# Slot attention of a two-layer decoder on one core: units of four heads, projection weights cut into fp32r parts, masks and scales moved from VectorE to ScalarE and GpSimd

## The reference, cut to what matters

```python
h = layernorm(x)
q, k = rope(h @ Wq.T), rope(h @ Wk.T)        # 16 heads x 128
v, g = h @ Wv.T, h @ Wg.T                    # 16 heads x 128
s = clip(h @ Ws1.T @ Ws2.T + bs2, -32, 32)   # 16 heads x 64 slots
z = cumlogsumexp(s, over time); es = exp(s); enz = exp(-z)
A = where(mask, q @ k.T * DK**-0.5, 0)
ok = enz * (A @ es)
qv = softmax(ok)
W2 = where(mask, (qv * enz) @ es.T, 0)
o = W2 @ v
x = x + (o * rsqrt(mean(o*o) + eps) * g_norm * silu(g)) @ Wo.T
```

## Time and profile before

| | |
|---|---|
| times of three runs | 2183.06, 2193.24, 2196.49 us (median 2193.24) |
| the profiled execution | 2183.35 us, span 2181.5 us |
| PE busy in the span | 1842.2 us, 84% |
| DVE busy | 1384.4 us, 63% |
| ACT busy | 763.0 us, 35% |
| POOL busy | 338.7 us, 16% |

### The profile page before, as it was taken

The page is one execution under the profiler, slowest core; times in us unless marked ns, Lnnn a source line. Parts: engine busy times, 40 slices in busy tenths (PEclk is TensorE's granted clock), DMA queues, the critical chain, the costliest instruction groups (busy, mean ns, idle before and its releaser), DMA issues.

```text
span 2181.5 us, 30632 instructions
## 1 busy us (share of the span) xinstructions
PE 1842.2 (84%) x11622; PEld 1096.2 (50%) x11622; DVE 1384.4 (63%) x3057; ACT 763.0 (35%) x1191; POOL 338.7 (16%) x507
## 2 busy tenths in 40 slices
PE   6998898898875559898998988997697598999977
PEld 3677777676763213343433435564354244444446
DVE  6766675775644546778677834343556687888843
ACT  1122122122121204545545561342122155556652
POOL 1311111111202100102011003242110011311110
PEclk9999999999996759999999997999798799999989
DMA  6000000000007270722707207363712136465200
GB/s 223 1 1 1 1 1 1 0 1 0 1 1 184 98 97 31 122 30 88 95 30 125 28 2 293 126 215 130 128 35 38 44 42 117 74 96 68 28 1 20
DMA packets 86747, 142.91 MB, mean 66 GB/s; under 512 B 14229, under 2 KB 56345, under 8 KB 86602
## 3 DMA queue, kind: packets, MB, share of 16 engines
q1 hardware_dynamic: 72418, 116.12, 25.7%
q10 hardware_dynamic: 12312, 19.71, 3.2%
q0 software_dynamic: 1872, 5.13, 0.6%
HBM read 108.35 MB, written 32.03 MB: 64 GB/s over the span
## 4 chain that ended last, share of the span: by engine, by line
PE 61%; DVE 19%; DMA 7%; issue 6%; ACT 3%; SPq 2%; POOL 1%; ACTq 1%; another core or an unknown queue 0%; POOLq 0%; DVEq 0%
PE bank L1054 8%; PE bank L1014 7%; PE bank L1033 6%; PE bank L1369 5%; PE bank L1704 5%; PE bank L556 4%; PE bank L625 3%; PE bank L1723 2%; PE bank L547 2%; DVE xa_part_max L1127 2%; PE bank L599 2%; PE bank L2113 2%; DMA xa_k_parts<-xa_parts 1%; DMA xa_qst<-xa_q_parts 1%; DVE gsa_enz L716 1%
## 5 line engine op out<-in xcount | busy, mean ns | idle before, releaser
L1127 DVE TENSOR_REDUCE xa_part_max<-bank 128x1 f32<-128x448 f32 (+1 forms) x512 | 273.8, 569 | 85.7 <-PE bank L1014 80.5
L1088 ACT ACTIVATE xa_e<-bank 128x1024 f32<-128x1024 f32 (+1 forms) x208 | 212.5, 1022 | 145.1 <-PE bank L1033 143.0
L1088 ACT ACTIVATE ca_e<-bank 128x1024 f32<-128x1024 f32 (+2 forms) x208 | 196.4, 956 | 102.4 <-PE bank L1033 93.8
L1127 DVE TENSOR_REDUCE ca_part_max<-bank 128x1 f32<-128x400 f32 (+1 forms) x384 | 205.9, 570 | 36.6 <-PE bank L1014 32.8
L1014 PE MATMUL bank<-xa_kst,xa_qst 122*128 122x448 bf16 (+1 forms) x512 | 172.0, 361 | 48.9 <-issue 24.9
L1014 PE MATMUL bank<-ca_kst,ca_qst 125*128 125x400 bf16 (+2 forms) x512 | 161.2, 351 | 25.5 <-DMA ca_qst<-ca_q_parts 11.8
L1033 PE MATMUL bank<-xa_qst,xa_kst 128*128 128x256 bf16 (+1 forms) x832 | 129.8, 279 | 21.5 <-DMA xa_qst<-xa_negT 21.5
L1054 PE MATMUL bank<-xa_e,xa_vaug 128*17 128x256 f32 (+2 forms) x1792 | 142.8, 394 | 1.0 <-ACT xa_e L1088 0.6
L1054 PE MATMUL bank<-ca_e,ca_vaug 128*17 128x256 f32 (+2 forms) x1664 | 126.2, 376 | 8.9 <-ACT ca_e L1088 8.0
L813 POOL TENSOR_TENSOR gsa_qk<-gsa_qk,gsa_rot 128x512 f32<-128x512 f32 x64 | 82.8, 1294 | 298.8 <-DVE gsa_rot L727 298.8
L1014 PEld LDWEIGHTS bank<-xa_kst,xa_qst 122*128 122x128 bf16 x512 | 48.8, 99 | 159.0 <-DVE xa_part_max L1127 83.9
(11 more groups left out here) (337 smaller groups left out, 3528.3 us busy)
## 6 DMA issues: line engine op xcount, KB each, us to landing
xa_kst<-xa_k_parts SPq DMA_DIRECT2D x96, 200.1 KB, 8.8
ca_kst<-ca_k_parts SPq DMA_DIRECT2D x96, 200.1 KB, 7.5
xa_k_parts<-xa_parts SPq DMA_DIRECT2D x8, 1200.8 KB, 6.0
ca_k_parts<-moe_ctx_parts SPq DMA_DIRECT2D x8, 1200.8 KB
moe_gu<-in_expert_gate_up SPq DMA_DIRECT2D x8, 1024.0 KB
shared<-in_ctxT_split ACTq DMA_DIRECT2D x4, 1601.0 KB, 7.8
moe_ctxT<-in_ctxT SPq DMA_DIRECT2D x8, 800.5 KB, 8.0
ca_cv<-in_ctx ACTq DMA_DIRECT2D x4, 1536.0 KB
```

The costliest lines, as they stand in the source:

```text
L1088: e.activation(self.e[m % 3][0:rows, :, first:T], banks[m % 2][0:rows].rearrange("p a (h t) -> p (a h) t", t=T)[:, :, first:T], ACT.Exp, s ...
L1127: e.tensor_reduce(top, work[:, 0:hi - lo], AX.X, ALU.max).then_inc(*reduced(t, *step))
```

## The change

- Sixteen units of four heads of one sequence. The order of the units is turned round: all four sequences with the first four heads, then with the next. The weights of a head group are loaded as it comes up (`w_raw`), and each is cut once per group into two fp32r parts: ACT rounds (`w_hi`), POOL subtracts (`w_lo`). The same is done with hT (`h_split`). wo comes and is scaled by group too, and the output projection is added to x after each unit, 32 additions where there were 8.
- The projections qk, v and gate are done by `product`, three fp32r matmuls for each fp32 one.
- `et` is made by transposing es on PE and copying it on ACT, where it was a matmul, a clip on DVE and an exp on ACT.
- The scores of `a` and `w2` are copied out of PSUM by ACT, and POOL zeroes the masked entries in place (`seen`, an affine_select over the two diagonal blocks). `scale` is done by POOL.
- `rr` comes once per unit, on 8 columns where there were 32, and ends with a copy to `rr4`: 14 small instructions on DVE, sixteen times.
- The outputs run two units behind the scores, `rr`, `scale`, `ot` and `wo` three behind. qk has three buffers (two before), enz and esT three, clip one.
- The first layer norm goes sequence by sequence inside the list, so the first projection waits for two tiles and not for eight.

In the diff the parts that only rename or re-index are left out.

```diff
-        G8, G4 = 8, 4
-        GSA_UNITS = [(b, g) for b in range(B) for g in range(HEADS // G8)]
-        wq, wk, wv, wg = (sb(n, [P, DC, HT]) for n in ("wq", "wk", "wv", "wg"))
+        G4 = 4
+        GROUPS = HEADS // G4
+        GSA_UNITS = GROUPS * B
+        w_parts = {key: [sb(f"w{key}{i}", [P, 2, DC, GK]) for i in range(2)] for key in LINEAR}
+        w_raw = {key: sb(f"w{key}", [P, DC, GK]) for key in LINEAR}
+        h_parts = sb("h_parts", [P, 2, DC, B * T])
...
+            def scores(m):
+                for s in range(G4 * m, G4 * (m + 1)):
+                    if s < G4 * GSA_UNITS:
+                        yield "qk", s
+                    if 0 <= s - 4 < G4 * GSA_UNITS:
+                        yield "ok", s - 4
+                    if 0 <= s - 2 < G4 * GSA_UNITS:
+                        yield "a", s - 2
+                    if s % G4 == 0 and 0 <= m - 2 < GSA_UNITS:
+                        yield "sm_exp", m - 2
+                if 0 <= m - 1 < GSA_UNITS:
+                    yield "sm_max", m - 1
...
+            def behind(m):
+                done = list(outputs(m - 2)) if 0 <= m - 2 < GSA_UNITS else []
+                if 0 <= m - 3 < GSA_UNITS:
+                    yield from finish(m - 3)
+                yield from done[:4]
+                if 0 <= m - 3 < GSA_UNITS:
+                    yield from project(m - 3)
+                yield from done[4:]
...
+            for m in range(GSA_UNITS + 3):
+                yield from weave(list(weave(list(scores(m)), list(ahead(m)))), list(behind(m)), lead=4)
-        gsa_front, gsa_back, gsa_clips = Ring(3, (hT_ready, "norm_turn", 0, NT - 1)), Ring(3), Ring(2)
+        gsa_front, gsa_back = Ring(3), Ring(3)
...
-                    for s, w in enumerate((wq, wk)):
-                        for c in range(DC):
-                            m = e.matmul(ps[:, s * T:(s + 1) * T], w[:, c, hd * DK:(hd + 1) * DK], hT[:, c, b * T:(b + 1) * T],
-                                         start=(c == 0), stop=(c == DC - 1))
+                    for s, key in enumerate("qk"):
+                        q.wait_ge(w_lo, g, key)
+                        m = product(e, ps[:, s * T:(s + 1) * T], [(w_parts[key][g % 2][:, :, c, k * DK:(k + 1) * DK], h_parts[:, :, c, b * T:(b + 1) * T])
+                                                                  for c in range(DC)])
...
+                elif kind == "a":
+                    q.wait_ge(a_mm, n)
+                    e.activation(aT[n % 2][:], bank[j][:, 0:3 * P], ACT.Copy, scale=scale).then_inc(*a_copied(*step))
...
-                elif kind == "a":
-                    e.scalar_tensor_tensor(aT[n % 2][:], bank[places[0][0]][:, 0:3 * P], scale, causal[:], ALU.mult, ALU.mult).then_inc(*a_ready(*step))
-                elif kind == "w2":
-                    e.tensor_tensor(w2T[s][:], bank[5 + places[0][0]][:, 0:3 * P], causal[:], ALU.mult).then_inc(*w2_ready(*step))
...
                     rsqrt(q, e, rr[:], rv[:], rt[:])
                     q.wait_ge(dve_own)
+                    e.tensor_copy(rr4[:], rr[:]).then_inc(*rr_ready(n))
...
+            def seen(t):
+                part = t[:].rearrange("p (k t) -> p k t", k=3)[:, 0:3:2, :]
+                return e.affine_select(part, part, [[0, 2], [1, P]], ALU.is_ge, 0.0, base=0, channel_multiplier=-1)
...
+                elif kind == "w_split":
+                    e.tensor_tensor(w[:, 1].bitcast(F32R), w_raw[key][:], w[:, 0], ALU.subtract).then_inc(*w_lo(n, key))
+                elif kind == "a":
+                    q.wait_ge(a_copied, *step)
+                    seen(aT[n % 2]).then_inc(*a_ready(n))
+                elif kind == "w2":
+                    q.wait_ge(w2_copied, *step)
+                    seen(w2T[s]).then_inc(*w2_ready(n, s))
+                elif kind == "scale":
+                    q.wait_ge(rr_ready, n)
+                    e.tensor_tensor(o4, o4, rr4[:, i, :].unsqueeze(2).broadcast_to([P, G4, DK]), ALU.mult).then_inc(*scaled(n, i))
```

More of the change, by code:

```diff
@@ L378, in build @@
         ones = causal[:, P:2 * P]
[L379 to L382, removed]
+        es = [sb(f"es{i}", [P, TB, GM]) for i in range(2)]
+        enz = [sb(f"enz{i}", [P, TB, GM]) for i in range(3)]
+        esT = [sb(f"esT{i}", [P, G4 // 2, T]) for i in range(3)]
+        v = [sb(f"v{i}", [P, TB, GK]) for i in range(2)]
@@ new lines, in project @@
+            def project(n):
+                for i in range(TB):
+                    yield "ot", n, i
+                    yield "wo", n, i
+                if n // B == GROUPS - 1:
+                    yield from norm_steps(1, n % B)
+            def behind(m):
[6 more added lines that the diff above has]
+                yield from done[4:]
@@ L504, in gsa_pe @@
                 kind, n, *rest = step
-                if kind in ("rr", "scale", "sm_max", "sm_exp", "norm_stats", "norm"):
-                    continue
-                free = places[0][1] if places else None
-                ps = places and (bank[5 + places[0][0]] if kind in ("z", "w2", "gate", "o", "ot", "wo", "norm_turn") else bank[places[0][0]])
                 if kind == "norm_turn":
@@ L641, in gsa_act @@
                     i, = rest
[L642 removed]
                     if n >= 2:
[L644 to L657 removed]
+                        q.wait_ge(o_mm, 2 * (n - 2) + 1)
@@ L658, in gsa_act @@
+                    q.wait_ge(v_mm, n, i)
+                    e.copy(v[n % 2][:, i, :], bank[j]).then_inc(*v_ready(*step))
+                elif kind == "a":
+                    if n >= 2:
+                        q.wait_ge(ok_mm, n - 2)
+                    q.wait_ge(a_mm, n)
+                    e.activation(aT[n % 2][:], bank[j][:, 0:3 * P], ACT.Copy, scale=scale).then_inc(*a_copied(*step))
                 elif kind == "sm_exp":
-                    half, = rest
-                    part = sm[n % 2][:, :, half * G4 * SLOTS:(half + 1) * G4 * SLOTS]
@@ L671, in gsa_act @@
                     e.copy(zb[SLOTS:P, 1, :], ps[SLOTS:P, 0:T]).then_inc(*z_ready(*step))
+                elif kind == "w2":
+                    s, = rest
+                    if n:
+                        q.wait_ge(o_mm, n - 1)
+                    q.wait_ge(w2_mm, n, s)
+                    e.copy(w2T[s][:], bank[5 + j][:, 0:3 * P]).then_inc(*w2_copied(*step))
                 elif kind == "gate":
```

533 lines of the change are left out of this document (261 added, 272 removed).

## The result

The change makes the program slower by 0.9%: 2205.5 us median where the kernel before took 2183.1 in the same comparison, ratio 1.0088, 95% interval 1.0060 to 1.0116. That is within the 1% band that got 0.50, but on the other side of it: the forecast was 2187 us against a median of 2193, a ratio of 0.997. The 2205.5 us lie inside the forecast's own range of 2165 to 2210 only because that range was set against a median that came out 10 us lower later, and because errors of both signs met in the sum.

The account below looks back on a forecast made before the run. The prediction took PE to set the pace; its savings would return as waits. Start 17.5, first units 66, thirteen units 504 and end 73 gave a 660 us stage against 666, so 2187 us for the program, range 2165 to 2210.

Parts of the forecast that it names:

- the 1% band that got 0.50: Whole program: chance 0.50 that the time changes by no more than about 1% (22 us), what a measurement can tell.
- the forecast's own range: Whole program: 2165 to 2210 us, from errors of half a microsecond per wait.
- 17.5 + units 0 to 2: 66 us: Stage's beginning: first q and k end at about 17.5 us, then units 0 to 2 take 66 us with lags.
- One unit and 73 us: Stage's end: one unit, then 73 us for three rounds without projections: PE work 39, norms, rr and scale, waits, half clock.
- The mechanism: Steady units: PE waits for exp before cs and for its bank behind rr and reciprocal; 37.5 us, 28.8 of them work.
- The clock term of 2 us a unit: Steady units: a half-clock stretch in each costs about 2 us of PE's work, making units 39.5 and 38 us.
- 52 us were forecast for fp32r: q and k, gate and v on PE: twelve fp32r products replace eight fp32 records, 0.41 us less, 128 times.
- 59 were forecast: PE over the stage: work falls by 59 us, 52 from the fp32r projections and 7 from et as transposes.
- DVE 408 us against 373: DVE over the stage: 429 us less 104 for masks, scale and clips, plus 48 for rr and x additions, gives 373.
- The sum of the prediction: Stage: 17.5 + 66 + 504 + 73 = 660 us against 666, with PE's savings coming back as sixteen waits in the units.
- (a): Steady units: DVE's bunch holds PE cheaply, clock stays 1.0, POOL's product falls outside rr; 42 us less, 2145 us, chance 0.22.
- (c): Steady units: slower because the clock stays down, two half-clock stretches per unit; 44 us more, 2231 us, chance 0.12.

Follow-up runs that it names:

- both edits: Changed kernel with first norms of sequences 1 to 3 ahead of round 0 and next-stage norm transposes one round later; ratio 0.9935 to the kernel before.
- e9: Kernel of e3 with rr behind the reciprocal, scales ahead of the first gate, ot and wo behind the second gate; ratio 0.9801 to the kernel before.
- e5: Kernel of e3 with the causal masks of a and w2 back on DVE, without ACT's copies and POOL's selects; ratio 0.9937 to the kernel before.
- e14: Kernel of e9 with each projection as one fp32 matmul in place of three fp32r products; ratio 0.9943 to the kernel before.
- after: The changed kernel itself, without follow-up edits, against the kernel before; 2205.5 us, ratio 1.0088.
- e1: Changed kernel with the first norms of sequences 1 to 3 and their splits put ahead of round 0; ratio 0.9979 to the kernel before.
- e2: Changed kernel with the PE transposes of the next stage's norms one round later, the norms unmoved on DVE; ratio 1.0046 to the kernel before.
- e3: Changed kernel with the edits of e1 and e2 together; ratio 0.9935 to the kernel before.
- e7: Kernel of e3 with the norm transposes and h splits of sequences 1 to 3 put into round 0; ratio 0.9925 to the kernel before.

## Why the prediction was wrong

- **Beginning (the step that failed most).** "17.5 + units 0 to 2: 66 us". The first q and k were nearly right (the rotation behind them at 18.8), the three units took 97.8, 31.8 more. I had summed DVE's work, the norms in it, and added "lags", and gave PE no wait for the norms and the clock no fall. But norm, transposes, rounding and remainder are a chain through four engines, and the list puts the next unit's first q,k right behind it: 12.2 us from the first norm instruction on DVE (31.07) to the first product (43.28) for sequence 1, of which PE stands 9.25; for sequence 2 it stands 6.93, for sequence 3 0.90. With the chain ahead of the rounds unit 3 is reached 24.9 us sooner, at 91.7. The forecast had 83.5, so 8 us stay missed in that order too; that its three units then take 66.3 us is chance, since the norms are no longer in them.
- **End.** One unit and 73 us, 111 together; measured 122.8. The waits of the last three rounds were about as listed, 30.5 us against 30: norms of 3.67, 4.28 and 4.29 us (4.3 each), 5.98 behind an uncovered `rr` and 4.09 for POOL's product of the softmax, where I had `rr` twice (10), and 8 us of small ones (7). The missing 12 us are the norm in round 15 (waits of 1.72 and 2.96 us, which the sum leaves out) and some 7 that none of these waits holds. PE is busy 83.2 us there at a clock of 0.84; how the 7 divide between dearer products, the rest of round 15 and the half clock, for which I had 4, no run shows.
- **The units.** The mechanism was right: exp 1.98 (2.2), the collision with POOL 1.29 in place of 0.17 us (1.2 more), enz 2.76 to 3.13 (4.0). The size was not: 37.2 us against 38.8, 19 us over twelve units. The clock term of 2 us a unit was the error. Without it the forecast's units are 37.5 and 36, 36.8 in the mean. The middle had 27 us at the lower level in all (0.03 x 2 x 446), and units 7 and 11 show that such a stretch costs no time there. The rule of the Trainium skill, "TensorE: Matmul & The Clock Gate", Part 1, that the ramp is under 1% of a typical span, would be 4.5 us of these 446. The trace agrees with it in the middle, where the stretches cost 0 to 0.2 us a unit. The rule speaks of a whole span; at this stage's ends 70 of 221 us ran at 1.2 GHz, and it can't be carried over to them.
- **PE's work.** 52 us were forecast for fp32r, from a pitch of 0.1145 us. The pitch holds within a row of products (0.118), but a group behind another kind of step takes up to 0.2 more, and fp32 costs 1.72 to 1.73, not 1.78. It was mis-sized by 15 us or more, and hidden in the errors above. PE's busy time says the same: with both edits it is 526.1 us in the stage, at a clock of 0.96, 42 less than before at 0.95, where 59 were forecast.
- **DVE, ACT, POOL.** DVE 408 us against 373: some 24 of the 35 are L806 and L783 (1141 and 1230 ns in the mean, 0.17 and 0.69 us undisturbed), both long where they run beside an operation of POOL. ACT's copies 0.489 (0.5), POOL's selects 0.41 to 0.46 (0.42), scale 1.04 (1.27), POOL 239 (250). None of it decided.
- **Where the gain went.** Between heads 12 and 60 the change takes 29 us off: PE is busy 37 us less and idle 8 more. The sum of the prediction let 10 us through there and had the rest come back as waits in the units; it was given back at the two ends, 48 us.
- **The rivals.** In the middle the time lies half way between the forecast and (a): the clock cost nothing, as (a) has it, but POOL's product did fall into `rr`. (c) has the right sign for another reason: the half clock is at the ends, not twice in each unit.
- **Luck.** The stage was missed by 26 us and the program by less than the range allows because the 19 us of the units stood against 33 and 12 at the ends. The sign of the whole was wrong.

What the runs don't settle: why late transposes bring 10 us and not 12, and how much of the ends' cost is the clock and how much the waits, since no run changed one without the other. An estimate from PE's busy time gives the clock at most 10.8 of the 24.9 us at the beginning and 4.4 of the 10.6 at the end.

## What to carry to other kernels

A norm, a split or a load that is spread over rounds to start sooner is free only if its whole chain across the engines fits beside the work in between; walk that chain for the first and the last rounds by themselves, because there little covers it (waits of 3 to 6 us here), and the clock was at 0.84. Taking work off an engine (93 us from DVE) brought almost nothing while the order decided; moving the small instructions of `rr` (3.8 us in round 7) behind the one that frees a bank brought 1.3% of the program, but only together with their consumers: rr late alone cost 1.9%, the projection late alone 0.7%.

## What was not expected of the hardware

- An operation on 128x8 elements took 1.29 us, to 273.14, while POOL ran a product of two SBUF tiles from 271.82 to 273.11; in the mean of 16 units 1.141 us, in the neighbouring small ones 0.17. Moved to another place (e9) it met POOL's addition of a rotation and took 1.108 us in the mean.
- The rest of the program has the same instructions in all kernels, yet from the stage's end to the end of the span the profiled executions took from 1500.9 us (e5) to 1525.2 (e14), the changed kernel 1513.5; the runs don't show why. A difference of one profile's spans can be off by as much as the effect here; the stage's end is the better mark, and unit times repeat within 0.2 us where the order is the same (37.2 to 37.4 in after, e1, e2, e3 and e7).
